# ViT tower on one core: the loads and low parts that prepare three stages, in another order

## What is computed

```python
h = tok_ref(x, ...)                                   # 64 x 65 x 128
h = h + attn_ref(layernorm(h), ...)
h = h + ffn_ref(layernorm(h), ...)

def expert(x, p):                                     # D = 256, vmapped over 4 experts
    h = ln(relu(x @ ew1 + eb1) @ ew2 + eb2, eg, ebeta)
    q, k, v = split(h @ aiw + aib)
    h = attention(q, k, v) @ aow + aob
    mem = concat([lstm(h, wif, whf, bf), lstm(h[:, ::-1], wib, whb, bb)[:, ::-1]])
    g = sigmoid(relu(mem @ sw1 + sb1) @ sw2 + sb2) * tanh(relu(mem @ tw1 + tb1) @ tw2 + tb2)
    return ln(relu(g @ dw1 + db1) @ dw2 + db2, dg, dbeta)
out = einsum('ebsd,bse->bsd', experts(x), softmax(x @ router_w + router_b))
```

## Time and profile before

| what | value |
|---|---|
| runs | 4261.22, 4262.17, 4261.21 us; median 4261.22 us |
| the profiled execution, its own time | 4262.6 us |
| its span, first to last instruction | 4260.8 us |
| PE (TensorE matmul) | 3717.0 us, 87% of the span |
| DVE (VectorE) | 2842.7 us, 67% |
| ACT (ScalarE) | 2168.0 us, 51% |
| POOL (GpSimd) | 1294.8 us, 30% |
| DMA | 205.03 MB, mean 48 GB/s |

### The profile page before, as it was taken

The page is one execution under the profiler, slowest core; times in us unless marked ns, Lnnn a source line. Parts: engine busy times, 40 slices in busy tenths (PEclk is TensorE's granted clock), DMA queues, the critical chain, the costliest instruction groups (busy, mean ns, idle before and its releaser), DMA issues. The chain is left out here.

```text
span 4260.8 us, 98548 instructions
## 1 busy us (share of the span) xinstructions
PE 3717.0 (87%) x36068; PEld 2277.4 (53%) x36068; DVE 2842.7 (67%) x5019; ACT 2168.0 (51%) x4390; POOL 1294.8 (30%) x1080
## 2 busy tenths in 40 slices
PE   6779689979988988961999999999999948999998
PEld 5645346645655655640555555555555526666665
DVE  8956468848858857875666666666666654555555
ACT  4546347736755755765444444444444435555554
POOL 0027437726726735755000000000000004444443
PEclk8879789989989989985999999999999978999999
DMA  8910100010010010024211111111111131111111
GB/s 175 176 25 0 54 14 2 1 55 2 0 41 15 0 42 31 1 68 134 82 43 48 49 47 49 44 47 49 48 48 45 46 94 52 53 52 52 53 55 32
DMA packets 392891, 205.03 MB, mean 48 GB/s; under 512 B 151221, under 2 KB 386474, under 8 KB 392106
## 3 DMA queue, kind: packets, MB, share of 16 engines
q1 hardware_dynamic: 392094, 200.93, 18.4%
q10 hardware_dynamic: 652, 2.19, 0.1%
HBM read 145.55 MB, written 57.51 MB: 48 GB/s over the span
## 5 line engine op out<-in xcount | busy, mean ns | idle before, releaser
L1765 PE MATMUL banks<-l_w,l_xs 128*64 128x512 f16 x6240 | 721.0, 381 | 18.1 <-DVE l_xs L1813 17.1
L1765 PE MATMUL banks<-l_w,l_hs 128*64 128x512 f16 x6144 | 705.7, 379 | 1.7 <-DVE l_hs L1819 1.7
L1765 PEld LDWEIGHTS banks<-l_w,l_xs 128*64 128x64 f16 x6240 | 343.8, 110 | 333.4 <-issue 24.2
L1765 PEld LDWEIGHTS banks<-l_w,l_hs 128*64 128x64 f16 x6144 | 348.1, 110 | 316.9 <-DVE l_hs L1819 2.2
L175 POOL MEMSET h_ident<- 128x128 f32 x1 | 0.2, 204 | 1443.2 <-POOLq L80 1443.2
L966 POOL TENSOR_TENSOR ax_p<-ax_p,ax_ri 128x520 f32<-128x520 f32 (+1 forms) x256 | 320.0, 1251 | 273.5 <-DVE ax_ri L1163 273.5
L1870 DVE SCALAR_TENSOR_TENSOR l_gates<-banks,l_unscale,l_bias 128x1024 f32<-128x1024 f32 x260 | 333.7, 1283 | 97.8 <-PE banks L1765 97.2
L1926 ACT ACTIVATE l_gates<-l_gates 128x768 f32<-128x768 f32 x260 | 219.1, 843 | 350.6 <-DVE l_gates L1870 350.6
L2200 PE MATMUL banks<-h_mem,h_w 128*128 128x320 f16 x2496 | 358.6, 301 | 4.3 <-issue 4.3
L2495 ACT ACTIVATE h_work<-banks,h_bias,h_factor 128x320 f32<-128x320 f32 x312 | 192.3, 616 | 264.6 <-PE banks L2200 260.9
L2200 PEld LDWEIGHTS banks<-h_mem,h_w 128*128 128x128 f16 x2496 | 245.2, 98 | 97.9 <-issue 4.6
(11 more groups left out here) (310 smaller groups left out, 7236.7 us busy)
## 6 DMA issues: line engine op xcount, KB each, us to landing
image<-in_x_dram SPq DMA_DIRECT2D x192, 196.0 KB
l_x<-x_scratch SPq DMA_DIRECT2D x130, 256.0 KB, 3.0
mem_scratch<-l_hs SPq DMA_DIRECT2D x520, 64.0 KB, 1.9
h_mem<-mem_scratch SPq DMA_DIRECT2D x104, 320.0 KB, 3.7
x_scratch<-x_out SPq DMA_DIRECT2D x4, 4160.0 KB, 16.4
raw_in<-in_L_ffn_attn_in_w_dram SPq DMA_DIRECT2D x4, 768.0 KB, 4.7
h_scratch<-x_out SPq DMA_DIRECT2D x1, 2080.0 KB, 6.5
z_scratch<-z SPq DMA_DIRECT2D x1, 2080.0 KB, 11.9
```

The source lines that it names most:

```text
L1765: mm = pe.matmul(ps[d * HALF:(d + 1) * HALF, 2 * z + n, :], lhsT, w_of[e][:, d, kk, b, n * 512:(n + 1) * 512], start=(kk == 0 and turn_ == ...
```

## The change

The vector rows of the experts' stage are loaded by SP in the stage before, ahead of expert 0's weights; vec_rows moves into Early. In the LSTM's stage load_x goes from behind matrix 4 to behind matrix 8, and the biases of expert e go behind matrix 12 + e. In the head SP waits for v_in before its first load, and z2 goes from ScalarE's queue onto SP's, between the matrices of experts 2 and 3; VectorE makes the whole low part of every expert; its wait for gain and beta moves from ahead of b2c to behind the last low part; and ScalarE waits for the LSTM's saves before its first rounding.

```diff
@@ -145,10 +146,19 @@
         sb = lambda name, shape: ctx.enter_context(nc.sbuf_tensor(name, shape, F32))
         self.z = sb("z", [P, TOKENS])
         self.xo = sb("x_out", [P, SEQ, KD, IMAGES])
+        self.vec_rows = sb("x_vec_rows", [EXPERTS * NVEC, P])
         self.raw_w1 = sb("raw_w1", [P, D])
         self.raw_w2 = sb("raw_w2", [P, KD, D])
         self.raw_in = sb("raw_in", [P, KD, 3 * D])
         self.raw_out = sb("raw_out", [P, KD, D])
+
+    def load_vectors(self, sp, io, loaded):
+
+        for name, key in (("b1", "enc_b1"), ("b2", "enc_b2"), ("g", "enc_g"), ("beta", "enc_beta"),
+                          ("in_b", "attn_in_b"), ("out_b", "attn_out_b")):
+            at, k = VECTORS[name]
+            sp.dma_start(self.vec_rows[EXPERTS * at:EXPERTS * (at + k), :],
+                         io[key].rearrange("e (k p) -> (e k) p", p=P)).then_inc(loaded, 16)
 
     def load(self, sp, io, e, loaded):
 
...
@@ -1318,6 +1328,7 @@
 
         def spill(sp, normed):
 
+            early.load_vectors(sp, experts_io, shared.vectors_in)
             early.load(sp, experts_io, 0, shared.raw_loaded)
             sp.wait_ge(normed, BASE + WSTEPS)
             sp.dma_start(h1_dram, h[:, :]).then_inc(shared.spilled, 16)
...
@@ -1429,7 +1440,7 @@
         def _(pe):
             pe.wait_ge(ones, BASE + 3)
             pe.wait_ge(id_done, BASE + 1)
-            pe.wait_ge(consts, BASE + 16 * len(VECTORS))
+            pe.wait_ge(shared.vectors_in, BASE + 16 * len(VECTORS))
             pe.transpose(ps[:, 0, 0:EXPERTS * NVEC], vec_rows[:, :],
                          ident[0:EXPERTS * NVEC, 0:EXPERTS * NVEC]).then_inc(vec_turned, 1)
             with pe.Fori(0, EXPERTS) as e:
...
@@ -1566,11 +1577,6 @@
 
         @block.scalar
         def _(act):
-            for name, key in (("b1", "enc_b1"), ("b2", "enc_b2"), ("g", "enc_g"), ("beta", "enc_beta"),
-                              ("in_b", "attn_in_b"), ("out_b", "attn_out_b")):
-                at, k = VECTORS[name]
-                act.dma_start(vec_rows[EXPERTS * at:EXPERTS * (at + k), :],
-                              io[key].rearrange("e (k p) -> (e k) p", p=P)).then_inc(consts, 16)
             with act.Fori(0, EXPERTS) as e:
                 act.wait_ge(prepared, BASE + e + 1)
                 at = VECTORS["b1"][0]
...
@@ -1702,10 +1708,11 @@
                 if q >= STAGES:
                     sp.wait_ge(w_low, BASE + q - STAGES + 1)
                 load_lstm_matrix(sp, io, q, stage[q % STAGES], stage_in[q % STAGES])
-                if q == STAGES:
+                if q == 2 * STAGES:
                     sp.wait_ge(shared.x_saved, BASE + 16 * EXPERTS)
                     load_x(sp, 0, 0)
-                    for e in range(EXPERTS):
+                if q >= 2 * STAGES + EXPERTS:
+                    for e in (q - 2 * STAGES - EXPERTS,):
                         for d, name in enumerate(("lstm_b_f", "lstm_b_b")):
                             for to, frm, width in COLUMNS:
                                 sp.dma_start(bias[d * HALF:(d + 1) * HALF, e, to:to + width],
...
@@ -2076,8 +2082,11 @@
 
         @block.sync
         def _(sp):
+            sp.wait_ge(v_in, BASE + 16 * LOADED)
             for e in range(2, E):
                 load_head_matrices(sp, io, e, raw[e], raw_in[e])
+                if e == 2:
+                    sp.dma_start(h1[:, :], z2_dram).then_inc(z2_in, 16)
             for e in range(E):
                 sp.dma_start(gain[:, e, :], io["dec_g"][e].partition_broadcast(P)).then_inc(g_in, 16)
                 sp.dma_start(beta[:, e, :], io["dec_beta"][e].partition_broadcast(P)).then_inc(g_in, 16)
...
@@ -2123,10 +2132,6 @@
             pool.memset(residual[:, W:WT], 0.0).then_inc(ones, 1)
             pool.wait_ge(ones, BASE + 6)
             pool.wait_ge(id_done, BASE + 1)
-            for e in range(E):
-                pool.wait_ge(w_high, BASE + e + 1)
-                pool.tensor_tensor(w[:, e, 1, 0:OURS], raw[e][:, 0:OURS], w[:, e, 0, 0:OURS], ALU.subtract).then_inc(w_low, 1)
-
             def low(name, n, scaled, split):
 
                 pool.wait_ge(S[name + "_high"], BASE + n + 1)
...
@@ -2188,7 +2193,6 @@
             mm.then_inc(routed, 1)
             pe.wait_ge(sizing, BASE + SIZING * E)
             pe.wait_ge(w_low, BASE + E)
-            pe.wait_ge(w_low2, BASE + E)
             pe.wait_ge(id_done, BASE + 1)
 
             def group(name, e, m, bank, moving):
...
@@ -2283,7 +2287,6 @@
                                 ps[:, 1, E * at:E * (at + k)].rearrange("p (e k) -> p e k", k=k)).then_inc(vec_kept, 1)
             dve.wait_ge(v_in, BASE + 16 * LOADED)
             dve.wait_ge(prep_pe, BASE + 1)
-            dve.wait_ge(g_in, BASE + 32 * E)
             at, _ = HEAD_VECTORS["dec_b2"]
             dve.tensor_tensor(b2c[:, :], vec[:, :, at], ps[:, 0, 0:E], ALU.subtract).then_inc(prep, 1)
             dve.wait_ge(vec_kept, BASE + len(HEAD_VECTORS))
...
@@ -2293,7 +2296,7 @@
             def low_w(e):
 
                 dve.wait_ge(w_high, BASE + e + 1)
-                dve.tensor_tensor(w[:, e, 1, OURS:], raw[e][:, OURS:], w[:, e, 0, OURS:], ALU.subtract).then_inc(w_low2, 1)
+                dve.tensor_tensor(w[:, e, 1, :], raw[e], w[:, e, 0, :], ALU.subtract).then_inc(w_low, 1)
 
             for e in range(E):
                 here = raw[e]
...
@@ -2347,6 +2350,7 @@
                 if e:
                     low_w(e - 1)
             low_w(E - 1)
+            dve.wait_ge(g_in, BASE + 32 * E)
 
             def high(name, n, scaled, split, readers):
 
...
@@ -2535,7 +2539,6 @@
                               io[name].rearrange("e (k p) -> (e k) p", p=P)).then_inc(v_in, 16)
             act.dma_start(rw[:, :], io["router_w"]).then_inc(v_in, 16)
             act.dma_start(rb[:, :], io["router_b"].partition_broadcast(P)).then_inc(v_in, 16)
-            act.dma_start(h1[:, :], z2_dram).then_inc(z2_in, 16)
             act.wait_ge(ones, BASE + 2)
             act.wait_ge(vec_kept, BASE + len(HEAD_VECTORS))
             for e in range(E):
...
@@ -2545,6 +2548,9 @@
                     act.activation(raw[e][:, at:at + k * width], raw[e][:, at:at + k * width], ACT.Identity,
                                    scale=w_scale[:, e, n:n + 1]).then_inc(w_scaled, 1)
                 act.wait_ge(w_scaled, BASE + NW * (e + 1))
+                if e == 0:
+                    for saved in shared.saved:
+                        act.wait_ge(saved, BASE + SEQ * 32)
                 act.copy(w[:, e, 0, :], raw[e]).then_inc(w_high, 1)
                 if e == 1:
                     act.wait_ge(z2_in, BASE + 16)
```

More of the change, by code:

```diff
@@ L133, in __init__ @@
         self.spilled, self.raw_loaded, self.x_saved = sem("spilled"), sem("raw_loaded"), sem("x_saved")
+        self.vectors_in = sem("vectors_in")
         with nc.Block() as block:
@@ L1345, in experts_stage @@
         h = sb("x_h", [P, KD, TOKENS])
-        vec_rows = sb("x_vec_rows", [EXPERTS * NVEC, P])
+        vec_rows = early.vec_rows
         vec_all = sb("x_vec_all", [P, EXPERTS, NVEC])
@@ L1377, in experts_stage @@
         SIZING = 6
-        consts, id_zero, id_done, ones = sem("x_consts"), sem("x_id_zero"), sem("x_id_done"), sem("x_ones")
+        id_zero, id_done, ones = sem("x_id_zero"), sem("x_id_done"), sem("x_ones")
         vec_turned, vec_kept = sem("x_vec_turned"), sem("x_vec_kept")
@@ L2011, in head_stage @@
         w = sb("h_w", [P, EXPERTS, 2, at], F16)
-        OURS = PLACE["s2"][0]
         NW = len(PLACE)
@@ L2063, in head_stage @@
         raw_in = shared.head_in
-        centred, measured, most_turned, most_shared, sizing, w_scaled, w_high, w_low, w_low2 = [
+        centred, measured, most_turned, most_shared, sizing, w_scaled, w_high, w_low = [
             sem("h_" + n) for n in ("centred", "measured", "most_turned", "most_shared", "sizing", "w_scaled", "w_high",
-                                    "w_low", "w_low2")]
+                                    "w_low")]
         mem_in = [sem(f"h_mem_in{q}") for q in range(2)]
```

## The result

The changed kernel takes 4217.53 us, the median of four runs (4215.42 to 4223.96), beside 4261.22 us of the kernel before, the median of four runs on the same chip. The ratio is 0.9900, with a 95% interval of 0.9887 to 0.9912: 42.6 us faster, between 37.5 and 48.2. The direction was right, and so were two of the three terms. The range was not.

The account below looks back on a forecast made before the run. Stages run one after another, and small loads decide when work begins at three hand-overs. Gains of 7.7 (experts), 9.5 (LSTM) and 21.2 us (head) sum to 38.4, off the median 4261.22: 4222.8 us, range 4219.5 to 4232.

Parts of the forecast that it names:

- The long loops between these places: Loops between the three stage hand-overs (experts, LSTM, head): not edited, so their time stays; change forecast 0.
- a loop between the stages runs at another pace: Loops between the edited stages: one of three signs named as showing the prediction wrong; no size given.
- for the rest: Lower end of the range: 1 us taken off the best of all three terms, 4220.4 us, giving 4219.5.
- The experts' start: Experts' stage: vector rows loaded a stage earlier let the transpose start earlier; gain 7.7 us, between 5.9 and 8.2.
- Rival 3: Experts' stage: GpSimd's setup holds VectorE through a second instruction, 1.8 us beyond the term, 4224.6 us; chance 0.06.
- The LSTM's preparation: LSTM's preparation: matrix 5 issued earlier gains 10.8 us, less 1.3 for biases; gain 9.5 us, between 3 and 10.8.
- costs nothing: LSTM's preparation: load_x, a microsecond on SP, stands behind matrix 8 before matrix 9's buffer is free; cost nothing.
- adds nothing: LSTM's preparation: matrix 15 is as late as matrix 13, but meets a GpSimd already moved by as much; nothing added.
- Rival 2: LSTM's preparation: biases hold matrices 13 and 15 back, their data competing too; 6.8 us beyond the term, 4229.6 us; chance 0.10.
- The head: Head's preparation: earlier vector rows, moved beta wait and VectorE's whole low parts gain 21.2 us, between 16.5 and 21.8.
- Rival 1: Head: the vector rows land no earlier, so the whole chain is 4.7 us later, 4227.5 us; chance 0.15.
- Rival 4: Head: expert 3's matrices become the bound; unchanged from 29.9 us late, slower from 46.9 us late; chance 0.07.

Follow-up runs that it names:

- the first pause: The changed kernel with one more VectorE reduction ahead of the copy at line 1511, first product 0.6 us later: 4230.37 us.
- the four pauses: Unused VectorE reductions ahead of that copy: changed kernel delayed 0.6, 1.8, 3.0 us took 4230.37, 4220.97, 4221.55 us; kernel before delayed 1.9 us took 4257.89.

## Why the prediction was wrong, and in which step

**The step that failed** is "The long loops between these places are not edited, so their time stays." They are not edited, and three engines keep their busy time in them to 0.2 us, but TensorE's clock doesn't keep its stretches. The prediction had put the loops' change at nothing, and what that cost it is 5.6 us by the means of five profiles each. Its last sentence had named "a loop between the stages runs at another pace" as a sign of being wrong, but neither the sum nor a rival had a price for it. The stages gave 7.8, 7.7 and 21.3 us, 36.8 in all where 38.4 were forecast. With 5.6 us of the loops that makes 42.4 us off 4261.2, 4218.8 us, 1.3 above the measured median. The range ended below at the best of the three terms less 1 us "for the rest". That 1 us was too little, which the three runs at hand (4261.21 to 4262.17 us) did not tell: later runs of the unedited kernel took 4251.5 to 4268.5 us, and profiles of kernels whose loops start as before differ by up to 10.3 us in them. The distance to the range is small by luck: the LSTM's preparation gave 1.8 us less than forecast, and with its forecast gain the median would lie 3.8 us below the range (an estimate).

**The experts' start**, 7.7 forecast and 7.8 measured, with the transpose behind the units memset and the copy drawn out to the end of GpSimd's. The rule of the Trainium skill (SBUF — State Buffer, Who interferes with whom) gave the same 0.4 us, and the trace agrees in kind: the copy took 0.48 us and ended 0.03 us behind the memset, while in the kernel with the first pause, where it started behind the memset's end, it took 0.17. Rival 3, a second GpSimd instruction, didn't come. The six loads in the stage ahead took SP 2.0 us and cost no time there: up to the spill it takes 517.2 us in the mean of the five profiles with them and 517.4 in the five without.

**The LSTM's preparation**, 9.5 forecast and 7.7 measured. The 10.8 us of the early matrix came in full: with the loads out of the way the preparation is 131.5 - 120.7 = 10.8 us shorter. The price of the loads was mis-sized: 1.3 us was forecast for one slip at matrix 13, and three slips of 1.0 us came. The sentence on load_x, "costs nothing", looked only at when SP was free to issue matrix 9. It left out the data of load_x: with load_x ahead, matrix 9 took 7.0 us from its issue to its maximum, and with load_x behind the last matrix 5.2 us. The slack at line 1844 in that group was 0.8 us before. And "adds nothing" was wrong for matrix 15: GpSimd had moved, but the biases ahead of that matrix held its issue back by 1.2 us as well. Rival 2 had that cause and both matrices, with too high a price: 6.8 us beyond my term against 1.8, of which load_x, which it did not have, made about 1.0.

**The head**, 21.2 forecast and 21.3 measured, with each instant on the way within 0.2 us. Taking the edits apart gave the priced parts back: two GpSimd stalls of 5.00 and 3.94 us, and 7.7 us in all where 7.6 were worked out. The 4.06 us for 3840 columns are what the chain shows, but not what the prediction's working gives: three times 1.39 us is 4.17. Rival 1 is settled against by the transpose. The rows landed 2.65 us behind the last issue when they were alone, where it was 7.3 us beside SP's matrices; so most of the 7.3 was sharing, not the rows' own time. Rival 4 didn't come, as no wait for a matrix stands on VectorE.

## What to carry to other kernels

An edit that moves the start of a loop can change its time without touching it, where TensorE's clock falls and rises at hand-overs inside it. So compare such loops over several profiles, take their spread into the range, and test by pauses of several lengths: where one doesn't cost what it lasts, position is at work. Two of the four pauses here would not have shown it. Where a stage's start waits on a chain of small loads, find the last one that is waited for before others are moved; moving the first ones alone cost 5.4 us here. A load put ahead of a matrix costs its data too, not only its issue; behind the last matrix it was free.

## What the runs showed of the hardware that was not expected

The fourteen profiles have 42 loops of experts 0 to 2, with the same instructions in each. How long such a loop takes goes with the moment at which the granted clock came back to its upper level behind the expert's first product:

| clock back, us behind the first product | loops | they take, us | at the lower clock some 60 to 90 us later, us |
|---|---|---|---|
| 2.8 to 3.8 | 14 | 334.9 to 338.6 | 10.2 to 17.1 |
| 7.8 to 9.0 | 21 | 340.3 to 343.5 | 17.1 |
| 9.3 to 9.6 | 7 | 337.4 to 338.3 | 13.7 |

So the costly position isn't the one at which the clock comes back latest. From 9.0 to 9.3 us the loops become shorter by 2 us and more, and the clock is down for 13.7 and not 17.1 us some 60 to 90 us later. With the first pause all hand-overs were of the costly kind (1349.3 us of loops), in the changed kernel only the first one (1334.7). The total at the lower clock doesn't give the loops by itself: with the wait for beta put back it was 141.1 us, and the loops took 1337.5.

What fixes the position of the very first hand-over is not settled. The stage ahead takes 513.9 to 520.7 us in these profiles, with no edit that should matter, and a clock that varies as well. No run fixed that, so a rule from which the position could be worked out ahead was not found; pauses between 0 and 0.6 us, and beyond 3 us, were not tried.
